# Attention over targets: one-hots turned on TensorE, maxima in two bf16 parts; a table stored from ScalarE's DMA queue

## The chip, the cores and the metric

The kernel runs on one core of a Trainium2 chip. The metric is the device time of one execution in microseconds, the median of three runs. TensorE is called PE, VectorE DVE, ScalarE ACT, GpSimd POOL and SyncE SP, as in the profile.

## The reference, cut to what matters

Four graph layers run over 12,500 nodes with 64 features and 400,000 edges, whose targets (dst) are sorted. The change touches the preparation, which all layers share, and the first layer, an attention over the edges of each target with 4 heads:

```
xl = (x @ W_l + b_l).reshape(n, 4, 16);  xr = (x @ W_r + b_r).reshape(n, 4, 16)
e = (edge_attr @ W_e).reshape(-1, 4, 16)
g = leaky_relu(xl[src] + xr[dst] + e, 0.2)
logits = einsum('ehc,hc->eh', g, att)
amax = segment_max(logits, dst)
ex = exp(logits - amax[dst]);  denom = segment_sum(ex, dst)
alpha = ex / (denom[dst] + 1e-16)
out = segment_sum(xl[src] * alpha[..., None], dst)
```

## The kernel before

The nodes lie in 98 blocks of 128. The sorted edges are cut into NG = 880 groups of 512 edges (4 tiles of 128, T = 4), each within one block, and the first layer goes over the groups in order. All five engines run their own instruction stream over the groups, software-pipelined by hand: `stage(f, lag, ...)` in a `body(g)` runs step f for group g - lag. Loops are unrolled four times (SLOTS = 4), and only semaphores tie the engines together.

**One group.** SP loads the sources, the target keys (twice: one key per partition, and as a row `key16` sent to all 128 partitions) and 16 edge features. POOL gathers 4 x 128 rows of the table `tab0` by indirect DMA. PE turns the edge features (L991), ACT copies them (L1064), PE makes their products (`feature_rows`, L1012) and adds the rows of the targets with a one-hot (`key_rows`, L1019, 12 matmuls). DVE adds the gathered rows (L893) and forms the scores (L899 to L904).

**Two one-hots.** DVE makes both in `onehots`: `ohN` (nodes x edges, bf16) in one instruction from the loaded row (L882), and `oh` (edges x nodes, f32) in four from the keys (L886). `oh` is used by `node_sums` on PE (L1035), so DVE waits for the node sums four groups back (`s_acc`) before it writes its buffer again. ACT makes a penalty from `ohN` (L1069).

**Maxima.** ACT rounds the scores to bf16 (`hi`, L1080). PE turns them to 4 rows (`turn_scores`, L997), ACT copies them (L1095) with a permuted write, PE spreads each head's row over 128 partitions (`spread`, L1007; two heads in `spread_first`, two in `spread_others`, since there are two buffers), and DVE adds the penalty and reduces (L919, four per group). The new maximum `mn` is bf16 (L926). PE takes it back to the edges (`edge_maxima`, L1027, 4 matmuls), DVE subtracts (L937, L940), ACT takes the exponent (L1090), DVE multiplies the values (L945), PE sums by node (L1035) and DVE adds to ACC (L952, L955).

**Order on PE** in `body(g)`: spread_first(g-1), node_sums(g-2), feature_rows(g+1), turn_scores(g), spread_others(g-1), key_rows(g+1), edge_maxima(g-1), turn(g+2). **Order on DVE**: scores(g), onehots(g+2), maxima(g-1), keep(g-2), exponents(g-1), local_keys(g+3), gathered(g+1), values(g-1). **Order on ACT**: high_part(g), score_rows(g), kept(g+1), weights(g-1), rescale(g-1), features(g+2), penalty(g).

POOL also scatters, between the gathers, the sorted edge records (`scatter_fill`, L1495) that later layers read.

**The preparation** finds each edge's place. SP's one DMA queue takes, in this order, a 25 MB copy of edge features, 47 stores that fill the record array (L377, 144 MB), and 14 small stores of a table of tiles (L382, two for each of 7 pieces). DVE makes these pieces (L538 to L542) in two buffers; for piece c it waits (`s_tst`) until the stores of piece c-2 have landed. After the seventh piece DVE and PE place the edges (L561 to L569), and the phase ends.

Of the kernel before, what the change touches and what calls it, by code (L numbers as in the profile page):

```python
# [18 lines left out]
F32 = mybir.dt.float32  # L19
# [10 lines left out]
T = 4  # L30
# [116 lines left out]
def program(nc, x, src, dst, ea16, ea64, rowvec, wtab0, w_e, wtab1, w2, wtab2, watt_e, wgru, bgru, w1, w3, out):  # L147
# [11 lines left out]
    with ExitStack() as top:  # L159
# [134 lines left out]
        with phase() as ctx:  # L294
# [65 lines left out]
            with nc.Block() as block:  # L360
                @block.sync
                def _(sp):
# [12 lines left out]
                    for r in range(0, NG * T, RUN):  # L375
                        m = min(RUN, NG * T - r)
                        sp.dma_start(places[:, r:r + m, :], rinit[:, 0:m, :]).then_inc(s_rec, 16)  # L377
                    for c in range(NTS):
# [4 lines left out]
                    sp.wait_ge(s_rec, 16 * n_rec)  # L383
                    sp.wait_ge(s_eap, 16)
                    for q in range(2):
                        at_least(sp, s_tst[q], 32 * ((NTS + 1 - q) // 2))
# [382 lines left out]
        def target_attention():  # L769


            table, heads, width, n_val, order = tab0, HEADS, D, D, 0
            R = table.shape[1]
            PT = PT1
            VC = n_val // heads + 1
            att = rows[:, ROWS["att"]]
            with phase() as ctx:
                def sbl(name, shape, dt=F32):
                    return sb_in(ctx, f"t_{name}", shape, dt)

                def seml(name):
                    return sem_in(ctx, f"t_{name}")

                w = sbl("w_ea", [T * DE, T, width])
                key = sbl("key", [P, SLOTS, T], I32)
                idx = sbl("idx", [P, SLOTS, T, 1], I32)
                ea = sbl("ea", [P, SLOTS, T, DE])
                row = sbl("row", [P, SLOTS, GE], I16)
                N_LOADS = 4
                G, oh, Gv = in_place_of_h(ctx, ("t_G", R), ("t_oh", P), ("t_Gv", R))  # L790
                lo = sbl("lo", [P, T])
                ohN = sbl("ohN", [P, SLOTS, GE], BF16)
                pen = sbl("pen", [P, 2, GE], BF16)
                eaT = sbl("eaT", [T * DE, P])
                z = sbl("z", [P, T, width])
                za = sbl("za", [P, T, width])
                lg = sbl("lg", [P, 2, T, heads])
                hi = sbl("hi", [P, T, heads], BF16)
                lgT = sbl("lgT", [heads, GE], BF16)
                sel = sbl("sel", [heads, heads, P], BF16)  # L800
                junk = sbl("junk", [P, 2, GE], BF16)
                gm = sbl("gm", [P, heads])
                mn = sbl("mn", [P, heads], BF16)
                df = sbl("df", [P, heads])
                corr = sbl("corr", [P, 2, heads])
                dd = sbl("dd", [P, T, heads])
                V = sbl("V", [P, T, heads, VC])
                M = sbl("M", [P, NB + 1, heads])
                ps_ea = ps_in(ctx, "t_ps_ea", [P, 512])
                ps_lT = ps_in(ctx, "t_ps_lT", [P, 2 * GE], BF16)  # L810
                ps_z = ps_in(ctx, "t_ps_z", [P, T, width])
                n_lb = 2
                ps_lb = ps_in(ctx, "t_ps_lb", [P, n_lb, GE])
                ps_m = ps_in(ctx, "t_ps_m", [P, 512])
                ps_a = ps_in(ctx, "t_ps_a", [P, 512])
                s_w, s_mi = seml("ea_weights"), seml("maxima_set")
                s_ld = [seml(f"edges_landed{k}") for k in range(SLOTS)]
                s_g = [seml(f"gathered{k}") for k in range(SLOTS)]
                (s_wz, s_lo, s_oh, s_ohN, s_pen, s_eaP, s_eaT, s_z, s_add, s_kept, s_act, s_mul, s_lg, s_hi, s_lT, s_lTc, s_sel, s_mn, s_df,
                 s_mb, s_corr, s_me, s_d0, s_d, s_p, s_V, s_acc, s_sc, s_done) = (seml(n) for n in (  # L820
                    "ea_weights_zero", "local_key", "onehot", "onehot_nodes", "penalty", "ea_turned", "ea_ready", "edge_rows",
                    "rows_added", "gathered_kept", "activated", "weighted", "score", "score_high", "score_turned", "score_rows", "selector", "new_max",
                    "max_step", "max_stored", "rescale", "edge_max", "score_less_max", "exponent", "weight", "values", "group_sums",
                    "acc_rescaled", "group_done"))
                s_lb = [seml(f"scores_spread{h}") for h in range(heads)]
                s_gm = [seml(f"group_max{h}") for h in range(heads)]
                filler = scatter_fill(ctx, 2, 0, (1, 3), (2, 0), (1, 0), ROUNDS)

                def tile_of(a, t):
                    return a.rearrange("n (p t) -> n t p", t=T)[:, t, :]  # L830

                with nc.Block() as block:
                    @block.sync
                    def _(sp):
                        sp.wait_ge(s_wz, 1)
                        for t in range(T):
                            sp.dma_start(w[t * DE:(t + 1) * DE, t, :], w_e).then_inc(s_w, 16)

                        def body(g, k, r):
                            at_least(sp, s_lo, g - SLOTS + 1)  # L840
                            at_least(sp, s_ohN, g - SLOTS + 1)
                            settle(sp)
                            at_least(sp, s_g[k], r * (16 * T))
                            at_least(sp, s_eaP, g - SLOTS + 1)
                            settle(sp)
                            e = sp.value_load(goff[0:1, bass.ds(g, 1)], min_val=0, max_val=E)
                            sp.dma_start(idx[:, k, :, 0], srcp[bass.ds(e, GE)].rearrange("(p t) -> p t", p=P)).then_inc(s_ld[k], 16)
                            sp.dma_start(row[:, k, :], key16[bass.ds(e, GE)].partition_broadcast(P)).then_inc(s_ld[k], 16)
                            sp.dma_start(key[:, k, :], keyp[bass.ds(e + 1, GE)].rearrange("(p t) -> p t", p=P)).then_inc(s_ld[k], 16)
                            sp.dma_start(ea[:, k], eap[bass.ds(e, GE), :].rearrange("(p t) c -> p t c", p=P)).then_inc(s_ld[k], 16)  # L850
                        steps(sp, NG, body, fill=lambda k, r: filler.load(sp, k, r), filled=filler.rounds)

                    @block.gpsimd
                    def _(pool):
                        def body(g, k, r):
                            pool.wait_ge(s_ld[k], (r + 1) * (16 * N_LOADS))
                            at_least(pool, s_add, g - SLOTS + 1)
                            at_least(pool, s_kept, g - SLOTS + 1)
# [4 lines left out]
                        steps(pool, NG, body, fill=lambda k, r: filler.scatter(pool, k, r), filled=filler.rounds)  # L863
                        filler.landed(pool)

                    @block.vector
                    def _(dve):
                        dve.memset(w[:], 0.0).then_inc(s_wz, 1)
                        dve.tensor_copy(sel[:], bcast(ident[0:heads, 0:heads], 2, P)).then_inc(s_sel, 1)
                        dve.memset(M[:], -LOW).then_inc(s_mi, 1)  # L870
                        dve.wait_ge(s_mi, 1)

                        def local_keys(g, k, r):
                            dve.wait_ge(s_ld[k], (r + 1) * (16 * N_LOADS))
# [1328 lines left out]
```

## Time and profile before

| | us |
|---|---|
| median of 3 runs (lowest to highest) | 25825.76 (25818.92 to 25836.37) |
| the profiled execution: its own time | 25656.45 |
| its span | 25654.3 |
| PE, DVE, ACT, POOL busy in it | 19085.9, 16571.8, 6762.4, 16256.9 |

The span is one execution from its first instruction to its last; busy time is an average over stages that have different limits. The preparation fills about the first 1050 us, the first layer's attention some 7.8 ms from 1312 us on.

### The profile page before, as it was taken

To read this page: it belongs to the slowest core of one execution; us is meant where nothing else is said; L and a number is where in the kernel's file an instruction comes from. 1 tells how busy PE (TensorE), PEld (TensorE's weight loads), DVE (VectorE), ACT (ScalarE), POOL (GpSimd) and SP (SyncE) were. 2 spreads that over 40 slices of the span, in tenths; PEclk is the share of its full clock that TensorE was granted. 3 is DMA by queue.
4 is the path that set the end of the run, shared out by engine and by line. 5 is a ranking of instruction groups with operands and counts; after the bars stand their busy time and mean duration, and the time that the engine had idled before them with its cause. 6 is when DMAs were issued, how large, how long until landed. Compare 5 with 4: busy or idle time off the path is not lost. (4 is left out here: it accounts for less than half of the span.)

```text
span 25654.3 us, 556495 instructions
## 1 busy us (share of the span) xinstructions
PE 19085.9 (74%) x100300; PEld 12086.3 (47%) x100301; DVE 16571.8 (65%) x59093; ACT 6762.4 (26%) x22440; POOL 16256.9 (63%) x16941
## 2 busy tenths in 40 slices
PE   3578888888888859999999987888888863333334
PEld 1244444444444435555555654666666633333332
DVE  4878888888888864444444556777777654444444
ACT  0033333333333322222222213444444311111111
POOL 0067777777777727777777643666666617777772
PEclk7755555555555555555555557999999855555555
DMA  7032332222233423333333365888888823333332
GB/s 300 5 62 57 57 57 57 57 57 57 57 57 57 57 37 75 76 75 76 75 75 76 70 51 95 132 131 131 129 132 132 117 35 59 59 59 59 59 59 22
DMA packets 3333220, 1984.04 MB, mean 77 GB/s; under 512 B 2469132, under 2 KB 2942196, under 8 KB 3325904
## 3 DMA queue, kind: packets, MB, share of 16 engines
q1 hardware_dynamic: 2735346, 1137.99, 22.6%
q0 software_dynamic: 597808, 845.34, 20.4%
q8 instruction: 21, 0.34, 0.0%
q14 instruction: 45, 0.37, 0.0%
HBM read 1667.63 MB, written 342.49 MB: 78 GB/s over the span
## 5 line engine op out<-in xcount | busy, mean ns | idle before, releaser
L861 POOL DMA_INDIRECT H<-tab,t_idx x3520 | 3405.6, 967 | 2300.0 <-DMA t_ea<-eap 1227.6
L1212 POOL DMA_INDIRECT H<-tab,a_rs x3520 | 3374.7, 959 | 1965.0 <-issue 1193.7
L1571 POOL DMA_INDIRECT H<-tab,m_idx x3520 | 3350.1, 952 | 1654.6 <-issue 1014.7
L1751 POOL DMA_INDIRECT g_G<-tab,g_rs x3232 | 3054.1, 945 | 1520.4 <-issue 944.5
L1495 POOL DMA_INDIRECT rec<-PT,posi x3125 | 3059.9, 979 | 1460.2 <-issue 1224.4
L1817 PE MATMUL g_ps_a<-g_zr,g_oh 128*128 128x64 f32 x6464 | 1586.4, 427 | 2620.3 <-ACT g_zr L1801 2011.6
L1817 PEld LDWEIGHTS g_ps_a<-g_zr,g_oh 128*128 128x128 f32 x6464 | 1438.7, 327 | 2768.6 <-issue 1903.5
L919 DVE CUSTOM_DVE_ANT_0 t_junk<-t_ps_lb,t_pen 128x512 bf16<-128x512 f32 x3520 | 2292.3, 689 | 555.9 <-PE t_ps_lb L1007 257.3
L1007 PE MATMUL t_ps_lb<-t_lgT,t_sel 4*128 4x512 bf16 x3520 | 1894.7, 603 | 498.5 <-DVE t_gm L919 468.6
L1671 PEld LDWEIGHTS m_ps_a<-m_Sx,H 128*128 128x128 f32 x7040 | 1565.6, 327 | 1416.0 <-issue 1415.3
L1035 PEld LDWEIGHTS t_ps_a<-t_V,H 128*128 128x128 f32 x7040 | 1567.5, 328 | 1367.1 <-issue 1367.1
L1035 PE MATMUL t_ps_a<-t_V,H 128*128 128x68 f32 x7040 | 1718.4, 426 | 590.8 <-DVE t_V L945 313.9
L1095 ACT COPY t_lgT<-t_ps_lT 4x512 bf16<-4x512 bf16 x880 | 1163.3, 1322 | 3499.2 <-PE t_ps_lb L1007 3498.5
L1781 DVE TENSOR_TENSOR ACC<-ACC,g_ps_a 128x64 f32 x3232 | 715.6, 221 | 1899.6 <-DVE ACC L1781 1524.0
L1671 PE MATMUL m_ps_a<-m_Sx,H 128*128 128x65 f32 x7040 | 1731.5, 424 | 0.5 <-ACT m_Sx L1694 0.5
L1645 PE MATMUL m_ps_m<-m_zT,w_sb 64*64 64x512 f32 x1760 | 1729.2, 1084 | 0.1
L1610 DVE TENSOR_TENSOR m_z<-m_ps_z,H 128x256 f32<-128x256 f32 x880 | 373.8, 425 | 2034.8 <-DMA H<-tab,m_idx 1300.5
L1603 DVE TENSOR_TENSOR_SCAN m_S<-H,m_S,m_ps_m 64x512 f32<-64x512 f32 x879 | 1116.1, 1270 | 795.9 <-PE m_ps_m L1645 795.8
L1317 PE MATMUL a_ps_z<-a_w_ea,a_eaT 64*128 64x288 f32 x3520 | 1101.9, 434 | 550.1 <-DVE a_z L1235 535.5
L1356 PE MATMUL a_ps_w<-PT,identb 128*128 128x432 bf16 x3524 | 1235.7, 358 | 0.0
L1689 ACT COPY m_zT<-m_ps_t 64x512 f32<-64x512 f32 x880 | 509.8, 579 | 2690.9 <-PE m_ps_t L1638 2687.2
L1638 PE MATMUL m_ps_t<-ident,m_zr 128*64 128x128 f32 x3520 | 925.3, 417 | 296.0 <-ACT m_zr L1699 294.7
(344 smaller groups left out, 37049.3 us busy)
## 6 DMA issues: line engine op xcount, KB each, us to landing
a_rs<-rec SPq DMA_DIRECT2D x880, 164.0 KB
rec<-H SPq DMA_DIRECT2D x46, 3116.0 KB
g_rs<-rec SPq DMA_DIRECT2D x3232, 41.0 KB
t_row<-key SPq DMA_DIRECT2D x880, 128.0 KB
m_row<-key SPq DMA_DIRECT2D x880, 128.0 KB
H<-startp SPq DMA_DIRECT2D x880, 128.0 KB
a_row<-keyc SPq DMA_DIRECT2D x880, 128.0 KB
PT<-in_ea SPq DMA_DIRECT2D x625, 160.0 KB
```

Source lines behind the costliest of these rows:

```text
L861: pool.indirect_dma_start(G[:, k, t, :], None, table, bass.IndirectOffsetOnAxis(ap=idx[:, k, t, :], axis=0)).then_inc(s_g[k], 16)
L919: dve.tensor_tensor_reduce(junk[:, h % 2], ps_lb[:, h % n_lb], pen[:, k % 2], 1.0, -LOW, ALU.add, ALU.max, gm[:, h:h + 1]).then_inc(s_gm[h ...
L1007: pe.matmul(ps_lb[:, h % n_lb], sel[:, h, :], lgT[:], start=True, stop=True).then_inc(s_lb[h], 1)
L1035: mm = pe.matmul(ps_a[:, 0:heads * VC], oh[:, k, t, :], V[:, t].rearrange("p h c -> p (h c)"), start=(t == 0), stop=(t == T - 1))
L1212: pool.indirect_dma_start(G[:, k % SLOTS, t, 0:R], None, tab2, bass.IndirectOffsetOnAxis(ap=rs[:, k, t, 1:2], axis=0)).then_inc(s_g[k % SL ...
L1356: pe.matmul(ps_w[:], identb[:], PT[:, 0, 0:3, :].rearrange("p s c -> p (s c)"), start=True, stop=True)
L1495: pool.indirect_dma_start(rec, bass.IndirectOffsetOnAxis(ap=self.posi[:, j, t:t + 1], axis=0), rbi[:, j, t, :], None).then_inc(self.s_sc[j ...
L1571: pool.indirect_dma_start(G[:, k, t, :], None, tab1, bass.IndirectOffsetOnAxis(ap=idx[:, k, t, :], axis=0)).then_inc(s_g[k], 16)
L1645: pe.matmul(ps_m[0:D, :], w[:], zT[:], start=True, stop=True).then_inc(s_msg, 1)
L1671: mm = pe.matmul(ps_a[:, 0:D + 1], ohL[:, k, t, :], Sx[:, t, :], start=(t == 0), stop=(t == T - 1))
L1751: pool.indirect_dma_start(G[:, k, t, :], None, tab3, bass.IndirectOffsetOnAxis(ap=rs[:, k, t, 1:2], axis=0)).then_inc(s_g[k], 16)
L1817: mm = pe.matmul(ps_a[:, q, t, 0:D], oh[:, q, t, :], zr[:, q, t, :], start=True, stop=True)
```

## The change

In the preparation the 14 stores of the table of tiles are issued by ACT instead of SP:

```diff
@@ sync
-                    for c in range(NTS):
-                        a, b = 512 * c, min(NT, 512 * c + 512)
-                        sp.wait_ge(s_ti, c + 1)
-                        for o in range(2):
-                            sp.dma_start(tiles[o:o + 1, a:b], ti[0:1, c % 2, o, 0:b - a]).then_inc(s_tst[c % 2], 16)
                     sp.wait_ge(s_rec, 16 * n_rec)
                     sp.wait_ge(s_eap, 16)
+                @block.scalar
+                def _(act):
+                    for c in range(NTS):
+                        a, b = 512 * c, min(NT, 512 * c + 512)
+                        act.wait_ge(s_ti, c + 1)
+                        for o in range(2):
+                            act.dma_start(tiles[o:o + 1, a:b], ti[0:1, c % 2, o, 0:b - a]).then_inc(s_tst[c % 2], 16)
```

`target_attention()` becomes `attention(layer, order, table, heads, width, we, n_val)`, called once, as `attention(0, 0, tab0, HEADS, D, w_e, D)`; its parts for other layers are not used. The row load is gone (3 loads instead of 4). DVE makes only the one-hot `ohb` (bf16, edges x nodes); PE turns it, and ACT makes the turned one-hot, the penalty and the f32 copy. Scores and maxima are carried as a high and a low bf16 part:

```diff
@@ DVE
-                            dve.tensor_scalar(ohN[:, k], row[:, k], base_node[...], pcol[:], ALU.subtract, ALU.is_equal).then_inc(s_ohN, 1)
                             dve.wait_ge(s_lo, g + 1)
-                            at_least(dve, s_acc, g - SLOTS + 1)
+                            at_least(dve, s_ohT, g - 1)
+                            at_least(dve, s_oh32, g - 1)
                             for t in range(T):
-                                ins = dve.tensor_scalar(oh[:, k, t, :], iota_b[:], lo[:, t:t + 1], None, ALU.is_equal)
+                                ins = dve.tensor_scalar(ohb[:, q, t, :], iota_b[:], lo[:, t:t + 1], None, ALU.is_equal)
+                        def split(g, k, r):     # after onehot(g+2), before maxima(g-1)
+                            dve.wait_ge(s_lp0, g + 1)
+                            dve.tensor_tensor(lgp[:, :, 1, :], lg[:, k % 2], lgp[:, :, 0, :], ALU.subtract).then_inc(s_lp, 1)
@@ DVE maxima
                             dve.tensor_tensor(mn[:], m_old, gm[:], ALU.max).then_inc(s_mn, 1)
                             dve.wait_ge(s_mn, g + 1)
+                            at_least(dve, s_me, g)
+                            dve.tensor_copy(mnp[:, 0], mn[:]).then_inc(s_mh, 1)
                             dve.tensor_tensor(df[:], m_old, mn[:], ALU.subtract).then_inc(s_df, 1)
                             dve.wait_ge(s_df, g + 1)
                             dve.tensor_tensor(m_old, mn[:], mn[:], ALU.max).then_inc(s_mb, 1)
+                            dve.wait_ge(s_mh, g + 1)
+                            dve.tensor_tensor(mnp[:, 1], mn[:], mnp[:, 0], ALU.subtract).then_inc(s_ml, 1)
@@ PE turn
+                            pe.wait_ge(s_oh, g + 1)
+                            at_least(pe, s_pen, g)
+                            for t in range(T):
+                                mm = pe.transpose(ps_oh[:, t, :], ohb[:, q, t, :], identb[:])
+                            mm.then_inc(s_ohT, 1)
@@ PE turn_scores
-                                mm = pe.transpose(ps_lT[0:heads, ...], hi[:, t, :], identb[:])
+                                mm = pe.transpose(ps_lT[0:2 * heads, ...], lgp[:, t]..., identb[:])
@@ PE edge_maxima
-                            pe.wait_ge(s_mn, g + 1)
+                            pe.wait_ge(s_mh, g + 1)
+                            pe.wait_ge(s_ml, g + 1)
                             for t in range(T):
-                                mm = pe.matmul(ps_m[...], tile_of(ohN[:, k], t), mn[:], start=True, stop=True)
+                                for i in range(2):
+                                    mm = pe.matmul(ps_m[...], ohN[:, k, t, :], mnp[:, i], start=(i == 0), stop=(i == 1))
@@ ACT
-                            act.activation(pen[:, k % 2], ohN[:, k], ACT.Copy, bias=-LOW, scale=LOW).then_inc(s_pen, 1)
+                        def copies(g, k, r):    # last in ACT's body, for group g+2
+                            act.wait_ge(s_ohT, g + 1)
+                            at_least(act, s_me, g - SLOTS + 1)
+                            act.copy(ohN[:, k], ps_oh[:, 0:T]).then_inc(s_ohN, 1)
+                            act.activation(pen[:, k], ps_oh[:, 0:T], ACT.Copy, bias=-BIG, scale=BIG).then_inc(s_pen, 1)
+                            at_least(act, s_acc, g - SLOTS + 1)
+                            act.wait_ge(s_oh, g + 1)
+                            act.copy(oh[:, k], ohb[:, q]).then_inc(s_oh32, 1)
-                            act.copy(lgT[:].rearrange("h (p t) -> h t p", t=T), ps_lT[0:heads, 0:GE].rearrange(...))
+                            act.copy(lgT[:], ps_lT[0:2 * heads, 0:T * P]).then_inc(s_lTc, 1)
```

The selector of `spread` has 8 rows instead of 4, two of them one, so that each head's high and low part are added.

## Rows read from the trace of the kernel before

**Rows 1.** First and last start of the node sums' matmuls, by source line:
```profile
L1035 PE MATMUL t_ps_a<-t_V,H x7040: 421/421/478, 1338.0 to 9143.1; 128*128 128x68 f32 x196
```
**Rows 2.** Windows: length, busy us (x instructions) by engine, PE clock, DMA share, GB/s:
```profile
4000.00:5000.00 1000.00, 819.29 (x3947) 448.94 (x3946) 803.72 (x2928) 320.99 (x903) 710.79 (x733) 0.50 0.30 57
10000.00:11000.00 1000.00, 932.34 (x4522) 577.25 (x4522) 497.31 (x1361) 214.64 (x530) 758.65 (x792) 0.50 0.38 75
16500.00:17500.00 1000.00, 861.37 (x6601) 627.32 (x6599) 771.08 (x3385) 423.26 (x1960) 683.87 (x714) 0.96 0.82 130
```
**Rows 3.** Waits of DVE, 4000 to 6000 us: total us, times, longest:
```profile
DVE H L886 <- PE t_ps_a L1035: 136.1, 225, 0.6
DVE t_junk L919 <- issue: 61.1, 113, 0.9
```
**Rows 4.** PE's timeline, one group: start, us, engine, line, operation, count, [idle before]:
```profile
5031.50 0.30 PE L1027 MATMUL t_ps_m<-t_mn,t_ohN 128*128 128x4 bf16 x4
5031.66 0.40 PE L991 MATMUL t_ps_ea<-ident,t_ea 128*64 128x128 f32 x1
5031.99 1.03 PE L1007 MATMUL t_ps_lb<-t_lgT,t_sel 4*128 4x512 bf16 x2
5033.84 1.95 PE L1035 MATMUL t_ps_a<-t_V,H 128*128 128x68 f32 x8 [0.82 <-DVE t_V L945]
5035.72 1.22 PE L1012 MATMUL t_ps_z<-t_w_ea,t_eaT 64*128 64x256 f32 x2
5036.86 0.59 PE L997 MATMUL t_ps_lT<-identb,t_hi 128*4 128x128 bf16 x4
5037.81 1.12 PE L1007 MATMUL t_ps_lb<-t_lgT,t_sel 4*128 4x512 bf16 x2 [0.36 <-DVE t_gm L919]
5039.20 0.97 PE L1019 MATMUL t_ps_z<-PT,t_ohN 128*128 x12 [0.26 <-issue]
5040.29 0.30 PE L1027 MATMUL t_ps_m<-t_mn,t_ohN 128*128 128x4 bf16 x4
```
**Rows 5.** DVE's timeline in the same group:
```profile
5035.90 0.88 DVE L886 TENSOR_SCALAR H<-iota_b,t_lo 128x128 f32<-128x128 bf16 x4 [0.60 <-PE t_ps_a L1035]
...
5038.57 0.69 DVE L919 CUSTOM_DVE_ANT_0 t_junk<-t_ps_lb,t_pen 128x512 bf16<-128x512 f32 x1 [0.29 <-PE t_ps_lb L1007]
...
5039.19 0.69 DVE L919 CUSTOM_DVE_ANT_0 t_junk<-t_ps_lb,t_pen 128x512 bf16<-128x512 f32 x1
...
5040.07 0.16 DVE L926 TENSOR_TENSOR t_mn<-t_M,t_gm 128x4 bf16<-128x4 f32 x1 [0.19 <-issue]
5040.27 0.17 DVE L929 TENSOR_TENSOR t_df<-t_M,t_mn 128x4 f32<-128x4 bf16 x1
...
5041.93 0.42 DVE L945 TENSOR_TENSOR t_V<-H,t_V 128x256 f32<-128x256 f32 x1
```
**Rows 6.** Two groups of ACT by line: shapes, count | busy us, mean ns | idle before:
```profile
L1095 ACT COPY t_lgT<-t_ps_lT 4x512 bf16<-4x512 bf16 x880 | 1163.3, 1322 | 3499.2 <-PE t_ps_lb L1007 3498.5 <-PE t_ps_lT L997 0.7
L1689 ACT COPY m_zT<-m_ps_t 64x512 f32<-64x512 f32 x880 | 509.8, 579 | 2690.9 <-PE m_ps_t L1638 2687.2 <-issue 3.7
```
**Rows 7.** Waits of PE in the second layer, 12000 to 14000 us:
```profile
PE m_ps_z L1653 <- issue: 28.1, 75, 0.4
```
**Rows 8.** The preparation, DVE's timeline around its long wait:
```profile
288.68 0.43 DVE L542 CAST ti<-fo 128x512 int32<-128x512 f32 x1
...
295.28 0.43 DVE L542 CAST ti<-fo 128x512 int32<-128x512 f32 x1
...
506.33 0.69 DVE L538 TENSOR_SCALAR ti<-ps_all 128x512 int32<-128x512 f32 x1 [210.23 <-DMA tiles<-ti]
```
**Rows 9.** The preparation: a window (columns of rows 2), the record stores and the last placing step:
```profile
300.00:500.00 200.00, 0.00 (x0) 0.00 (x0) 0.00 (x0) 0.00 (x0) 0.00 (x0) 0.50 1.00 430
L377 SPq DMA_DIRECT2D rec<-H x47: 433/6526/42002, 81.3 to 439.0; - x47
L569 DVE COPY_PREDICATED PT<-mask,ps_all x196: 1331/1888/2439, 566.2 to 1045.9; 128x2048 f32<-128x2048 int16 x98, 128x1077 f32<-128x1077 int16 x98
```

More of the change, by code:

```diff
@@ L767, in _, with attention @@
                         steps(act, NB, body, 2)
-        def target_attention():
-            table, heads, width, n_val, order = tab0, HEADS, D, D, 0
+        def attention(layer, order, table, heads, width, we, n_val):
             R = table.shape[1]
-            PT = PT1
+            PT = PT2 if layer == 2 else PT1
             VC = n_val // heads + 1
-            att = rows[:, ROWS["att"]]
+            v0 = R - n_val
+            banks = 1 if T * width <= 512 else 2
+            tpb = T // banks
+            att = rows[:, ROWS["att"]] if layer == 0 else rows[:, ROWS["w_att2"]]
@@ L815, in target_attention @@
[L815 to L830, printed above, removed]
+                ps_oh = ps_in(ctx, f"ps_oh{layer}", [P, 2 * T, P], BF16)
+                ps_ea = ps_in(ctx, f"ps_ea{layer}", [P, 512])
+                ps_lT = ps_in(ctx, f"ps_lT{layer}", [P, 2 * T * P], BF16)
@@ new lines, in attention @@
+                ps_z = ps_in(ctx, f"ps_z{layer}", [P, banks, 512])
+                n_lb = min(heads, 2)
+                ps_lb = ps_in(ctx, f"ps_lb{layer}", [P, n_lb, T, P])
+                ps_m = ps_in(ctx, f"ps_m{layer}", [P, 512])
+                ps_a = ps_in(ctx, f"ps_a{layer}", [P, 512])
+                zv = [ps_z[:, b, 0:tpb * width].rearrange("p (t c) -> p t c", t=tpb) for b in range(banks)]
+                s_w, s_mi, s_eac = seml("ea_weights"), seml("maxima_set"), seml("ea_together")
@@ L832, in target_attention @@
+                s_lb = [seml(f"scores_spread{h}_") for h in range(heads)]
+                if layer == 0:
+                    filler = scatter_fill(ctx, 2, 0, (1, 3), (2, 0), (1, 0), ROUNDS)
+                else:
+                    filler = None
+                s_gm = [seml(f"group_max{h}_") for h in range(heads)]
                 with nc.Block() as block:
@@ L968, in body @@
                                 blocks[1] = block_of(g - 1)
+                            stage(split, 0, NG, *at)
                             stage(maxima, 1, NG, *at)
@@ L1077, in high_part @@
                         def high_part(g, k, r):
+                            q = k % 2
+                            if layer:
+                                act.wait_ge(s_lg0, g + 1)
+                                at_least(act, s_d0, g - 1)
+                                act.activation(lg[:, q], ss[:], ACT.Identity, bias=rows[:, ROWS["b_att2"]]).then_inc(s_lg, 1)
                             act.wait_ge(s_lg, g + 1)
                             at_least(act, s_lT, g)
-                            act.copy(hi[:], lg[:, k % 2]).then_inc(s_hi, 1)
+                            act.copy(lgp[:, :, 0, :], lg[:, q]).then_inc(s_lp0, 1)
                         def rescale(g, k, r):
@@ L1099, in body @@
                             stage(score_rows, 0, NG, *at)
[L1100 removed]
+                            if layer == 0:
+                                stage(kept, -1, NG, *at)
                             stage(weights, 1, NG, *at)
@@ L1103, in body @@
                             stage(features, -2, NG, *at)
-                            stage(penalty, 0, NG, *at)
-                        for g in range(2):
-                            features(g, g, 0)
-                        kept(0, 0, 0)
-                        filler.first(act)
-                        pipeline(act, NG, body, 2, fill=lambda k, r: filler.keys(act, k, r), filled=filler.rounds)
+                            stage(copies, -2, NG, *at)
+                        features(0, 0, 0)
+                        copies(0, 0, 0)
+                        features(1, 1, 0)
+                        copies(1, 1, 0)
+                        if layer == 0:
+                            kept(0, 0, 0)
+                        if filler:
+                            filler.first(act)
+                            pipeline(act, NG, body, 2, fill=lambda k, r: filler.keys(act, k, r), filled=filler.rounds)
+                        else:
+                            pipeline(act, NG, body, 2)
         def source_attention():
```

219 lines of the change are left out of this document (133 added, 86 removed).

## The prediction

> **What bounds the kernel now.** I read the extent of the first layer's stage, then its windows, then DVE's and PE's waits, then one group on the two timelines, and last the preparation. All sums below are made against the profiled execution (span 25654.3 us, own time 25656.45); the median of the runs shown is 25825.76, 169 higher, and I put the difference on that.
>
> The stage runs from 1337.9 to 9143 us for 880 groups [rows 1]: 8.88 us a group, 30% of the span. In it PE is busy 82%, DVE 80%, POOL 71% and ACT 32% [rows 2]: no engine is full, so a loop of waits must set the pace. DVE waits in every group for the node sums, 136.1 us / 225 = 0.60 us [rows 3], and PE waits for DVE twice, 0.82 us for the values and 0.36 us for the first group maximum [rows 4]. So it is one ring over both: values, node sums on PE (1.95), one-hots on DVE, four maxima, values. Once in four groups DVE also loses up to 0.9 us for which it waits on nobody, 0.27 us a group on average [rows 3].
>
> In the preparation DVE stands still for 210.2 us until a tile store has landed [rows 8]. The window 300 to 500 us shows no instruction of a compute engine and DMA full at 430 GB/s [rows 9]. The small stores stand behind the record stores in SP's queue, the last of which starts at 439 us [rows 9]. This wait is on the path: the placing, which ends the phase at 1046 us, comes after it.
>
> **Part 1, the table of tiles.** The stores leave SP's queue. DVE's stall falls to what a store costs beside the records, which still keep DMA full until 506. The stores of piece c are needed two pieces on. A piece takes 6.6 us (288.68 to 295.28 [rows 8]), so a landing below that costs nothing. No row shows a small store beside a full queue. Bounds: from below 0 us left; from above the whole 210 us, if the stores still get through only when the records are done. The nearest row is the record store itself, 6.5 us median on the queue [rows 9]: if a small store waits for about one, a landing takes some 7 to 9 us and the five waits leave 5 to 10 us. I take 10 us left: **-200 us**. SP still waits for the records, but they end at 506 us, and the placing, moved from 1046 to some 846, covers them. ACT, which issues 14 stores, has nothing else in this stretch.
>
> The Trainium skill ("DMA: Bandwidth & Descriptors", "Queues, rings and completion order") says that each DMA engine takes turns between the queue rows that have work, a packet at a time, and SP and ACT own one row each; by that rule the stores pass the records, as I take it. The same page ("Issuing engines are not separate DMA queues") says that a second issuing engine saves only the time to issue; by that sentence alone part 1 would be worth nothing. No trace here has a transfer from ACT's queue, so neither is shown yet.
>
> **Part 2, the attention stage.** What goes: DVE's second one-hot (L882), the row load of 128 KB a group (DMA at 30% in this stage, cover enough [rows 2]: nothing), and the 0.60 us wait of DVE for the node sums, which moves to ACT, where the sums in question are long done. That breaks the ring, and a longer one takes its place, which I follow from one `edge_maxima` on PE to the next. It stays on PE up to the second pair of spreads, and goes over DVE from there:
>
> - edge_maxima, now 8 matmuls: 0.16 to the turn now [rows 4]; four take 0.30, so one more costs some 0.04: 0.16 + 0.16, with a second semaphore 0.35
> - four transposes of 128x128 bf16, new. The nearest row is turn_scores, also four with 128 moving columns, 0.59 from first start to last end [rows 4]. Taken by start to start: 0.48. Bounds 0.3 (loads and moves all overlap) and 0.9 (weights of 128 columns instead of 4 not hidden at all)
> - the feature turn to the first spread 0.33, the spread pair 1.03, a gap 0.05 [rows 4]
> - node sums to feature rows 1.88, feature rows to turn_scores 1.14 [rows 4]
> - turn_scores to the other spreads, wait left out: 0.95 now, of which 0.36 is a wait [rows 4]: 0.50 (the last end overlaps)
> - first of them to the third maximum 0.76 (37.81 to 38.57), third to fourth 0.62, fourth to `mn` 0.88 [rows 4, 5]
> - `mn` to the end of `ml`: DVE's small operations start 0.20 apart (40.07, 40.27 [rows 5]). Before, PE started 0.22 after `mn` began. Now `mh`, `df`, the stored maximum and `ml` lie between: 4 x 0.20 + 0.17 + 0.06 = 1.03
>
> The sum is 0.35 + 0.48 + 1.41 + 3.02 + 0.50 + 2.26 + 1.03 = 9.05 us. The same chain before, with its waits, is 8.79 (31.50 to 40.29 [rows 4]). In other words: 0.16 + 0.03 + 0.48 + 0.81 = 1.48 us are added to PE's chain, and some 1.22 come back, because PE no longer stands for the values (0.77) nor for the first maxima (0.45).
>
> The values must not be late in the new ring. They end 2.06 us after edge_maxima began (42.35 - 40.29 [rows 4, 5]), some 2.2 with the longer edge_maxima, and the spread pair ends 0.35 + 0.48 + 0.33 + 1.03 = 2.19 after it: just hidden. If the transposes are cheaper than I think, this wait returns and takes the gain.
>
> DVE has 7.14 us of work a group now [rows 2]. It loses one long operation and gains three of 0.17, so it stays near 7.2 of 9.05; its loop turn falls into this slack. PE's own loop turn, till now hidden behind waits, comes out: the nearest row is the second layer, 0.37 us a turn of four groups (28.1 / 75 [rows 7]), 0.1 a group. Another 0.05 is for waits that queue on PE behind `s_oh`, `s_pen` and `s_ohT`; behind these stand the feature turn and the spreads. New stage: 9.05 + 0.10 + 0.05 = 9.20 us a group, against 8.88: 0.32 x 880 = **+282 us**.
>
> ACT: now 2.85 us a group [rows 2]. It gains two copies out of PSUM and one in SBUF, 128x512 each, and moves the penalty; the score copy loses its permuted write. Prices: 0.58 for a plain copy of 512 f32 out of PSUM, 1.32 for the permuted bf16 one [rows 6]. I blame the permuted write for the 0.74 between them, so I take 0.6 each. The copies then end before DVE's scores do; `high_part`, which stands behind them on ACT and feeds DVE's new `split`, is not late. With 1.32 for the two copies out of PSUM it is; that is a rival.
>
> The Trainium skill ("ScalarE: Activation LUTs", "What ACT_TABLE_LOAD costs") gives an activation with immediate scale and bias 186 ns + 0.833 ns an element, for f32 and bf16 alike, 612 ns here. The plain copy agrees (579), the score copy does not (1322). By the rule alone the sum is mine; by the measured row it is rival B.
>
> Total: -200 + 282 = +82 us. 25825.76 + 82 gives 25908, which I round to **25900**.
>
> **The rivals.**
>
> A, faster: the new ring is no longer than the old one. Its place is PE between edge_maxima and the first spread. If transposes and the extra matmuls cost 0.35 together instead of 0.64, and `ml` starts 0.6 after `mn`, the group stays at 8.88 or falls to 8.8, and the 200 us of part 1 remain: 25560 to 25640. It decides below 0.23 us added per group (200 / 880). For it: 1.2 us of PE's waits are there to be used up. Against: four dependent starts of 0.20 can hardly be had for less.
>
> B, much slower: a bf16 read out of PSUM is what makes the score copy 1.32. Then turned one-hot and penalty cost 1.5 us more on ACT, `high_part` and `split` are late by some 0.6 to 0.8, turn_scores and the first maxima too, and a group takes some 9.7: 0.8 x 880 - 200 = +500, 26330. For it: nothing else on ACT reads bf16 there. Against: the permuted write is the more unusual part of that copy.
>
> C, much faster: PE's clock. It stands at 0.50 (1.2 GHz) throughout this stage, and at 0.50 with PE 93% busy in the second layer, but at 0.96 in the third, where PE is busy 86% [rows 2]. The transposes are more bf16 work. Should the stage go to 2.4 GHz, PE's 5.5 us of the ring halve, DVE becomes the bound at some 8.2: -0.7 x 880 - 200 = -800, 25000. Against: the new wait for `ml` opens a gap between key_rows and edge_maxima that was not there.
>
> D: the stores still wait for the records, all of part 1 is nothing, and the stage's +282 stand alone: 26110. The full DMA window [rows 9] speaks for it.
>
> **How the numbers follow.** My forecast (stage 9.1 to 9.4 a group, part 1 works; 25820 to 26080) 0.42, A 0.23, B 0.15, C 0.06, D 0.08, something slower still 0.06. Two runs of this kernel differ by under 0.2% (52 us), which is what counts as no change. The forecast's own range gives 0.30 slower, 0.12 same; A gives 0.20 faster, 0.03 same; C is faster, B, D and the rest slower: faster 0.26, same 0.15, slower 0.59. I move 0.06 from slower to faster for parts of the slack I may have missed: 0.32, 0.15, 0.53. The range takes A down to 25580 and B up to 26400.
>
> **What would show it.** Stall at L538 gone, placing done by about 850 us, and stores on ACT's queue: part 1 right. In the stage: no wait of DVE for `ps_a`, PE's waits for the values near zero, a wait of PE for `mnp` of some 0.8 us between key_rows and edge_maxima, group period 9.2. The copies out of PSUM at 0.6 on ACT, else B. Clock at 0.50, else C. I am wrong if the values still end last for the node sums, if the period stays under 9.1, or if the split is late.

## The result, and the profile after

The changed kernel takes 25441.5 us (median of 4 runs, 25411.0 to 25446.5), the kernel before 25822.3 beside it (25806.4 to 25836.4): a ratio of 0.985, interval 0.9833 to 0.9867, **381 us faster**. Forecast was 25900, 78 us slower, in a range from 25580: wrong in sign, and below the range.

The page of the profiled execution after (own time 25411.0 us), the span and one queue:

```profile
span 25409.4 us, 572084 instructions
...
q10 hardware_dynamic: 28, 0.03, 0.0%
```

The line q10 is new: ACT's queue, with 28 packets and 0.03 MB.

First the preparation, by line: the stores on ACT's queue (to [rows 8, 9]), the placing, and the node sums (to [rows 1]), with count, min/median/max ns, first and last start:

```profile
L387 ACTq DMA_DIRECT2D tiles<-ti x14: 200/236/481, 288.8 to 323.6; - x14
...
L572 DVE COPY_PREDICATED PT<-mask,ps_all x196: 1333/1886/2436, 358.9 to 837.9; 128x2048 f32<-128x2048 int16 x98, 128x1077 f32<-128x1077 int16 x98
...
L1114 PE MATMUL ps_a<-V,H x7040: 421/421/482, 1127.9 to 8713.5; 128*128 128x68 f32 x196
```

The stores go out as the pieces are made, the placing ends at 838 instead of 1046, and the attention stage begins at 1127.9 instead of 1338.0: 210 us sooner. The stage then lasts 7585.6 us instead of 7805.1: another 219.5 us, where I had forecast 282 more. The same two lines in the trace of before show what the old queue did:

```profile
L382 SPq DMA_DIRECT2D tiles<-ti x14: 214/253/8346, 445.7 to 530.9; - x14
...
432.08 13.56 SPq L377 DMA_DIRECT2D rec<-H  x2
445.69 70.12 SPq L382 DMA_DIRECT2D tiles<-ti  x8
```

The first store's data was ready at 289 [rows 8]; SP could issue it only at 445.7, after it had got rid of its last record store, and the stores that DVE waits for had landed at 506. So some 157 us passed before the issue, and 60 more while the records still filled DMA. DVE stood still from 296.1 on (506.33 - 210.23), so 150 of its 210 us lie before the issue.

Now the stage itself: one window (columns of [rows 2]), and PE's and DVE's waits from 4000 to 6000 us (total us, times, longest):

```profile
4000.00:5000.00 1000.00, 855.89 (x4976) 493.01 (x4976) 808.25 (x3246) 367.37 (x1159) 730.74 (x754) 0.50 0.22 44
```

```profile
PE ps_m L1106 <- DVE mnp L984: 274.2, 232, 1.3
PE ps_z L1096 <- issue: 13.6, 58, 0.2
...
DVE junk L975 <- PE ps_lb L1082: 204.4, 231, 1.2
```

No wait of DVE for the node sums, none of PE for the values; PE waits for `mnp` in every group, 1.18 us on average. The clock is still 0.50. The same on the timeline, one group from `edge_maxima` to `edge_maxima` (to [rows 4, 5]):

```profile
5001.57 0.16 DVE L981 TENSOR_TENSOR mn<-M,gm 128x4 f32<-128x4 f32 x1 [0.20 <-issue]
5001.77 0.17 DVE L984 CAST mnp<-mn 128x4 bf16<-128x4 f32 x1
5001.85 0.15 DVE L986 TENSOR_TENSOR df<-M,mn 128x4 f32<-128x4 f32 x1
5002.04 0.16 DVE L988 TENSOR_TENSOR M<-mn 128x4 f32 x1
5002.12 0.15 DVE L990 TENSOR_TENSOR mnp<-mn,mnp 128x4 bf16<-128x4 f32 x1
5002.23 0.23 DVE L1014 TENSOR_TENSOR ACC<-ACC,corr 128x68 f32 x1
...
5002.37 0.35 PE L1106 MATMUL ps_m<-mnp,ohN 128*128 128x4 bf16 x8 [1.31 <-DVE mnp L984]
...
5002.60 0.58 PE L1057 MATMUL ps_oh<-identb,ohb 128*128 128x128 bf16 x4
...
5002.98 0.42 PE L1065 MATMUL ps_ea<-ident,ea 128*64 128x128 f32 x1
...
5003.34 1.03 PE L1082 MATMUL ps_lb<-lgT,sel 8*128 8x512 bf16 x2
...
5003.64 0.41 DVE L1007 TENSOR_TENSOR V<-H,V 128x256 f32<-128x256 f32 x1
5003.68 0.58 ACT L1149 COPY ohN<-ps_oh 128x512 bf16<-128x512 bf16 x1
...
5004.16 0.59 ACT L1151 ACTIVATE pen<-ps_oh 128x512 bf16<-128x512 bf16 x1
...
5004.30 1.98 PE L1114 MATMUL ps_a<-V,H 128*128 128x68 f32 x8
...
5006.20 1.22 PE L1088 MATMUL ps_z<-w_ea,eaT 64*128 64x256 f32 x2
...
5007.35 0.59 PE L1072 MATMUL ps_lT<-identb,lgp 128*8 128x128 bf16 x4
...
5007.87 1.03 PE L1082 MATMUL ps_lb<-lgT,sel 8*128 8x512 bf16 x2
...
5008.65 0.69 DVE L975 CUSTOM_DVE_ANT_0 junk<-ps_lb,pen 128x512 bf16<-128x512 f32 x1 [1.16 <-PE ps_lb L1082]
...
5009.27 0.69 DVE L975 CUSTOM_DVE_ANT_0 junk<-ps_lb,pen 128x512 bf16<-128x512 f32 x1
...
5010.17 0.17 DVE L981 TENSOR_TENSOR mn<-M,gm 128x4 f32<-128x4 f32 x1 [0.20 <-issue]
...
5010.98 0.35 PE L1106 MATMUL ps_m<-mnp,ohN 128*128 128x4 bf16 x8 [1.32 <-DVE mnp L984]
```

It is the ring that I had drawn, in the order that I had drawn, with the period 8.61 instead of 9.20 us (8.59 to 8.70 over the four groups of a loop turn; the stage gives 8.62). From `mn` (5001.57) the two halves of DVE's little chain can be read: the high part of `mnp` after 0.20, but `df`, which needs only `mn`, already 0.08 behind it, and the low part 0.08 behind the stored maximum.

The two spans differ by only 245 us. The parts above make 430; 170 are lost again in the third layer, which the change does not touch: its node sums run 4968.1 us in the profiled execution before and 5138.0 after. Some 15 more are lost elsewhere.

```profile
L1349 PE MATMUL a_ps_a<-H x7040: 217/275/422, 15701.4 to 20669.5; 128*128 128x65 f32 x196
```

```profile
L1446 PE MATMUL a_ps_a<-H x7040: 217/275/422, 15285.0 to 20423.0; 128*128 128x65 f32 x196
```

### The profile page after: what moved, and what is told of

It is laid out like the page before. It is cut to its first block and busy times, and to the rows that moved or that the text cites. A ratio compares the mean times of both kernels' runs of the same rounds, so it can differ in the third digit from the quotient of the medians.

```text
span 25409.4 us, 572084 instructions
## 1 busy us (share of the span) xinstructions
PE 19250.5 (76%) x107313; PEld 12397.8 (49%) x107341; DVE 16439.5 (65%) x60853; ACT 7048.7 (28%) x24200; POOL 16250.5 (64%) x16941
## 5 line engine op out<-in xcount | busy, mean ns | idle before, releaser
L897 POOL DMA_INDIRECT H<-tab,idx x3520 | 3403.9, 967 | 2091.5 <-issue 1062.4
L975 DVE CUSTOM_DVE_ANT_0 junk<-ps_lb,pen 128x512 bf16<-128x512 f32 x3520 | 2292.5, 689 | 824.4 <-PE ps_lb L1082 779.0
L1114 PEld LDWEIGHTS ps_a<-V,H 128*128 128x128 f32 x7040 | 1567.2, 328 | 766.2 <-issue 766.2
L1082 PE MATMUL ps_lb<-lgT,sel 8*128 8x512 bf16 x3520 | 1828.9, 614 | 0.2 <-DVE gm L975 0.2
L1114 PE MATMUL ps_a<-V,H 128*128 128x68 f32 x7040 | 1731.0, 427 | 11.6 <-DVE V L1007 6.5
L1185 ACT COPY lgT<-ps_lT 8x512 bf16<-8x512 bf16 x880 | 506.1, 575 | 2962.5 <-PE ps_lb L1082 2961.3
```

Source lines behind the costliest of these rows:

```text
L897: pool.indirect_dma_start(G[:, k, t, :], None, table, bass.IndirectOffsetOnAxis(ap=idx[:, k, t, :], axis=0)).then_inc(s_g[k], 16)
L975: dve.tensor_tensor_reduce(junk[:, h % 2].rearrange("p t e -> p (t e)"), ps_lb[:, h % n_lb].rearrange("p t e -> p (t e)"), pen[:, k].rearr ...
L1082: pe.matmul(ps_lb[:, h % n_lb].rearrange("p t e -> p (t e)"), sel[:, h, :], lgT[:], start=True, stop=True).then_inc(s_lb[h], 1)
L1114: mm = pe.matmul(ps_a[:, 0:heads * VC], oh[:, k, t, :], V[:, t].rearrange("p h c -> p (h c)"), start=(t == 0), stop=(t == T - 1))
```

## The experiments

The runs were made in three groups, each with runs of the kernel before beside them: 1 to 4 (on the chip that the record numbers 15), 5 to 8, and 9 to 12 some 25 minutes later (both on the number 6). "Stage" is the extent of the node sums, first start to last start.

**1. The stores alone.** The kernel before, with the 14 stores issued by ACT as in the diff above.

> The kernel before, with only the 14 stores of the table of tiles issued from ScalarE's DMA queue. Theory (queue): the stores pass the record stores, DVE's stall of 210.2 us at the third piece is gone, the node sums of the first layer start at 1128 instead of 1338, the stage itself still takes 7805 us: -210 us. Rival (the same DMA engines are full, so the stores wait as before): no change. If the two parts don't add up, this and the next run show by how much.

25775.7 us against 25979.8: ratio 0.9925 (0.9908 to 0.9941), -204. The stage, by line:

```profile
L1038 PE MATMUL t_ps_a<-t_V,H x7040: 421/421/478, 1132.2 to 8935.4; 128*128 128x68 f32 x196
```

It begins 206 us sooner than [rows 1] and lasts as long (7803.2).

**2. The attention alone.** The changed kernel, with the stores back on SP.

> The changed kernel, with the 14 stores back on SyncE's queue: the attention part alone. Theory (ring): the stage takes 7586 us instead of 7805, 8.62 instead of 8.88 us a group, the stall of 210 us stays: -220 us. Rival (my recorded sum): the ring with its new terms is 9.2 us a group, +280 us.

25750.0 us: ratio 0.9918 (0.9902 to 0.9935), -230. Stage 7579.3 us, from 1337.8 on. DVE's waits in the preparation hold the old stall:

```profile
DVE ti L538 <- DMA tiles<-ti: 211.7, 1, 211.7
```

The two halves add: -204 and -230 make -434, and the profiled execution after gave -430 up to the end of this stage. The whole change measured -381, some 50 less; the third layer's time, which differs between executions, may hold that, but no run shows it. Both halves are gains, so the step that failed is the stage's sum.

**3. The old ring opened without the new one.** In the kernel before, only the f32 one-hot, which waited for the node sums, is made one body later, so that these are long done. Nothing goes to PE or ACT, no value is split (lines shortened):

```diff
-                        def onehots(g, k, r):   # both, for g+2
+                        def onehots(g, k, r):   # only ohN, for g+2
+                            dve.wait_ge(s_ld[k], (r + 1) * (16 * N_LOADS))
                             dve.tensor_scalar(ohN[:, k], row[:, k], ...).then_inc(s_ohN, 1)
+
+                        def onehots32(g, k, r): # s_lo, s_acc, four tensor_scalar
...
+                            stage(onehots32, -1, NG, *at)
...
-                            stage(local_keys, -3, NG, *at)
+                            stage(local_keys, -2, NG, *at)
```

> The kernel before, with the f32 one-hots made one body later on DVE (group g+1 instead of g+2 in body g, the local keys with them), so that the buffer that they overwrite was read a whole body ago; no work is added or removed, nothing is turned on PE, no parts are split. Theory (ring): the pace of before was the ring values -> node sums -> one-hots; with it broken DVE's wait for ps_a of 0.60 us is gone and the period falls from 8.88 to some 8.3 us (then POOL's 6.5 transfers a group of 1.27 us each, or DVE with some 8.0, is the bound): -500 us. Rival (the gain came from DVE having less to do and from the cheaper score copy): no change, 8.88 us a group.

25494.0 us: ratio 0.9818 (0.9802 to 0.9834), -486, twice what the change's whole attention part gives. Stage 7311.9 us, 8.32 a group. POOL's waits from 4000 to 6000 us, and the window:

```profile
POOL H L861 <- issue: 286.6, 940, 0.3
...
POOL rec L1500 <- issue: 182.9, 600, 0.3
```

```profile
4000.00:5000.00 1000.00, 852.32 (x4207) 472.86 (x4207) 843.63 (x3129) 346.55 (x965) 761.85 (x782) 0.50 0.33 61
```

DVE no longer waits for the node sums, so the old ring was what [rows 3, 4] said. What bounds now is, by its own time, an engine I had left out: POOL works 761.85 us of the window and stands 0.30 us between every two of its 782 indirect transfers, 235 us more. That is 997 of 1000. It hardly waits for anybody (7 us in 2000); at 6.5 transfers a group, 0.97 + 0.30 us each, it needs 8.3 us. No run takes transfers away, so this bound is read from the trace and not tested.

**4. The score copy.** In the kernel before, ACT writes `lgT` in order and reads PSUM permuted, instead of the reverse:

```diff
-                            act.copy(lgT[:].rearrange("h (p t) -> h t p", t=T), ps_lT[...].rearrange("h (t p) -> h t p", t=T))
+                            act.copy(lgT[:].rearrange("h (p t) -> h p t", t=T), ps_lT[...].rearrange("h (t p) -> h p t", t=T))
```

> The kernel before, with the copy of the turned scores on ScalarE walking its elements in the order of its output (written in a row, read from PSUM in strides) instead of the order of its input. Theory (the strided write is what cost 1.32 us against 0.58 of a plain copy): the copy takes about 0.6 us; off the ring it gains nothing, 8.88 us a group, no change within 0.2%. Rival (the copy is on the path from the spreads of one group to those of the next): 0.3 to 0.7 us a group less, -260 us or more. If the read's stride costs as much as the write's, the copy stays at 1.3 us and nothing can change.

25972.6 us: ratio 0.9999 (0.9989 to 1.0009), no change. The copy, by line:

```profile
L1095 ACT COPY t_lgT<-t_ps_lT 4x512 bf16<-4x512 bf16 x880 | 506.3, 575 | 3501.3 <-PE t_ps_lb L1007 3500.7 <-PE t_ps_lT L997 0.7
```

575 ns instead of 1322 [rows 6]: the permuted write made all of the difference. Still bf16 and still out of PSUM, so rival B's reason is refuted, and the copy is off the ring.

**5 to 8.** The same kernels as 9 to 12, in the second group of runs, 25 minutes earlier. In it all kernels ran 38 to 42% longer, the one before too (35563.6 us). In run 5 DVE stood still for 4.9 us on average about once a group (149 times, 735 us in all, from 4000 to 6000 us), in turns at two lines. No trace was kept of the kernel before beside these runs. Two of the stops, at one of the lines, two groups apart (timeline):

```profile
4002.40 0.17 DVE L996 TENSOR_TENSOR dd<-lg,ps_m 128x16 f32<-128x16 f32 x1 [4.92 <-remote]
...
4029.07 0.17 DVE L996 TENSOR_TENSOR dd<-lg,ps_m 128x16 f32<-128x16 f32 x1 [4.75 <-remote]
```

> The changed kernel, with DVE making the low part of the new maximum straight after the high part, ahead of the step and the stored maximum; nothing else moved. In the changed kernel edge_maxima starts 0.81 us after mn. Theory (the pace is now PE's ring, with this stretch of DVE in it): edge_maxima starts some 0.62 us after mn, the period falls from 8.62 to 8.43 us, the stage from 7586 to about 7420 us. Rival (PE or DVE is bound by its own work, or the values end last): the stage stays at 7586 within 20 us.

> The changed kernel, with PE turning the four one-hot tiles twice in a row (the same result written twice). In the changed kernel the four took 0.38 us from first start to the next instruction's. Theory (PE's ring without slack): the period rises by the whole of four more, 0.38 to 0.43 us, the stage to some 7930 to 7960 us. Rival (PE has slack ahead of the values, since edge_maxima starts late): less than half of that, below 7760 us. Should the added bf16 work raise PE's granted clock, it will stand above 0.50 in the stage and the period will fall.

> The changed kernel without the low part of the maxima: DVE does not make it, PE takes only the high part back to the edges (4 matmuls instead of 8) and does not wait for it. Theory (ring): edge_maxima starts 0.42 us after mn instead of 0.81, the ring is 8.62 - 0.39 - 0.05 = 8.18 us, but POOL's transfers allow no less than some 8.3 us a group (6.5 of 1.27 us): the stage takes 7300 to 7340 us, as in the kernel with the one-hot made later. Rival (the low part costs only its own 0.08 us on DVE): 7500 us or more.

> The kernel before with the two things that the runs point to and nothing else of the change: the f32 one-hots a body later on DVE, and the 14 stores of the table of tiles on ScalarE's queue. Theory: the gains add up, -486 and -204 us, that is -690 us or 2.65%, with the stage at 7312 us and the start of its node sums at 1132 us. Rival (the shift in time brings them into each other's way, or later stages give it back as they wait on POOL's records): less than -600 us.

Ratios: 0.999 (0.998 to 1.0001), 1.0215 (1.0195 to 1.0235), 0.9813 (0.9793 to 0.9832), 0.9715 (0.9699 to 0.9731). They have the order of the runs below, but with the stops none of the expected extents could be read, so the four were run again. The expectations below speak of "the chip of e5 to e8" and of stops "once per turn of its loop". The record has one chip number for both groups, so it isn't shown that the chip was another one, and a loop turn is four groups, so the stops come oftener.

**9. The low part sooner.** In the changed kernel the low part of the maximum is made right behind the high one:

```diff
                             dve.tensor_copy(mnp[:, 0], mn[:]).then_inc(s_mh, 1)
+                            dve.wait_ge(s_mh, g + 1)
+                            dve.tensor_tensor(mnp[:, 1], mn[:], mnp[:, 0], ALU.subtract).then_inc(s_ml, 1)
                             dve.tensor_tensor(df[:], m_old, mn[:], ALU.subtract).then_inc(s_df, 1)
```

> The kernel of e5 again: on the chip of e5 to e8 every engine stood still for some 5 us once per turn of its loop, in the kernel before too, which hid what the edit does; between those stops the period was 8.49 or 8.72 us, against 8.60 and 8.66 in the changed kernel. Theory (PE's ring, with DVE's stretch from mn to the low part in it): without the stops the stage takes about 7420 us, 8.43 us a group. Rival (another wait takes its place): 7540 to 7590 us.

25279.3 us against 25666.0: ratio 0.9855 (0.9835 to 0.9874), the changed kernel's own ratio. Stage 7599.4 us: my theory's gain is not there, and the rival's 7540 to 7590 is all but met. The timeline:

```profile
4015.51 0.16 DVE L981 TENSOR_TENSOR mn<-M,gm 128x4 f32<-128x4 f32 x1 [0.20 <-issue]
...
4015.71 0.17 DVE L984 CAST mnp<-mn 128x4 bf16<-128x4 f32 x1
4015.92 0.16 DVE L986 TENSOR_TENSOR mnp<-mn,mnp 128x4 bf16<-128x4 f32 x1
4016.00 0.15 DVE L988 TENSOR_TENSOR df<-M,mn 128x4 f32<-128x4 f32 x1
...
4016.18 0.36 PE L1106 MATMUL ps_m<-mnp,ohN 128*128 128x4 bf16 x8 [1.18 <-DVE mnp L984]
...
4017.71 0.41 DVE L1007 TENSOR_TENSOR V<-H,V 128x256 f32<-128x256 f32 x1
...
4018.36 1.55 PE L1114 MATMUL ps_a<-V,H 128*128 128x68 f32 x6 [0.18 <-DVE V L1007]
```

`edge_maxima` does begin sooner, 0.67 after `mn` instead of 0.81 (4016.18 - 4015.51). But three of the four operations behind `mn` now wait for the one just before, where it was two, so all that DVE does behind them comes later, the values too, and the node sums wait for the values. The four groups of a loop turn differ a little, so they are compared place by place: the values begin 2.21, 2.20, 2.39 and 2.24 us after `mn` against 2.06, 2.13, 2.31 and 2.17 in the changed kernel, and the node sums 2.73, 2.85, 2.90 and 2.75 against 2.73, 2.79, 2.82 and 2.74 (from 4006.95 and from 4000.30 us on). What `edge_maxima` gains is lost before the node sums.

**10. Turned twice.** In the changed kernel the four transposes are done twice:

```diff
-                            for t in range(T):
+                            for t in [*range(T), *range(T)]:
```

> The kernel of e6 again, for the same reason; between the stops its period was 9.00 to 9.04 us. Theory (PE's ring without slack): the stage takes 7930 to 7960 us, 0.39 us a group above the changed kernel's 8.62. Rival (slack ahead of the values): below 7760 us.

25597.6 us: ratio 0.9975 (0.9964 to 0.9985). Stage 7926.4 us, 0.39 a group above the changed kernel, for four transposes that took 0.38 to 0.43. On PE's timeline they stand in the ring at full price:

```profile
4025.96 0.35 PE L1106 MATMUL ps_m<-mnp,ohN 128*128 128x4 bf16 x8 [1.31 <-DVE mnp L984]
4026.18 1.01 PE L1057 MATMUL ps_oh<-identb,ohb 128*128 128x128 bf16 x8
4026.99 0.42 PE L1065 MATMUL ps_ea<-ident,ea 128*64 128x128 f32 x1
...
4034.96 0.35 PE L1106 MATMUL ps_m<-mnp,ohN 128*128 128x4 bf16 x8 [1.31 <-DVE mnp L984]
```

The period is 9.00, and PE's wait for `mnp` is unchanged although PE is behind by 0.4: DVE went along, as it must in a ring of both.

**11. No low part.** In the changed kernel `edge_maxima` uses the high part of the maximum alone; the low part is not made:

```diff
-                            dve.wait_ge(s_mh, g + 1)
-                            dve.tensor_tensor(mnp[:, 1], mn[:], mnp[:, 0], ALU.subtract).then_inc(s_ml, 1)
...
-                            pe.wait_ge(s_ml, g + 1)
```

> The kernel of e7 again, for the same reason; between the stops its period was 8.28 or 8.52 us. Theory (ring, then POOL's transfers as the floor): the stage takes 7300 to 7340 us, 8.3 us a group. Rival: 7450 us or more, as the mean of 8.28 and 8.52 says (8.40 x 880 = 7390 lies between).

25066.2 us: ratio 0.9771 (0.9752 to 0.9791). Stage 7405.0 us, 8.41 a group: between theory and rival, at 0.21 of the 0.3 expected. One group shows where the rest stayed:

```profile
4010.16 0.16 DVE L981 TENSOR_TENSOR mn<-M,gm 128x4 f32<-128x4 f32 x1 [0.20 <-issue]
...
4010.60 0.27 PE L1102 MATMUL ps_m<-mnp,ohN 128*128 128x4 bf16 x4 [0.96 <-DVE mnp L984]
...
4012.17 0.41 DVE L1005 TENSOR_TENSOR V<-H,V 128x256 f32<-128x256 f32 x1
...
4012.82 1.97 PE L1110 MATMUL ps_a<-V,H 128*128 128x68 f32 x8 [0.24 <-DVE V L1005]
```

`edge_maxima` begins 0.42 to 0.45 after `mn`, as expected, and PE's wait for `mnp` falls from 1.18 to 0.81 us:

```profile
PE ps_m L1102 <- DVE mnp L984: 191.8, 238, 1.0
```

But now the values come last: the node sums begin 2.44 to 2.68 after `mn` against 2.73 to 2.82, only 0.19 sooner on average.

**12. Both simple parts.** The kernel before with experiments 1 and 3: ACT's stores and the later f32 one-hot, nothing of the attention part of the change.

> The kernel of e8 again, for the same reason. Theory: the gains of e3 and e1 add up: -690 us or 2.65% (ratio 0.9735), the stage at 7312 us from 1132 us on. Rival: less than -600 us.

24959.9 us (24938.8 to 24979.7): ratio 0.973 (0.9714 to 0.9746), **-706**. The sum of 1 and 3 is -690: they add. The stage lasts 7312.3 us (1137.3 to 8449.6). It beats the kernel before and, by ratio, the changed one (0.985).

## Why the prediction was wrong

**Part 1 was right.** -200 forecast, -204 and -210 measured; the placing was done at 838 ("about 850"). The ten microseconds I left for the five waits were not there: DVE's only waits among the pieces are for PE. The Trainium skill ("DMA: Bandwidth & Descriptors", "Queues, rings and completion order") has each DMA engine take turns between the queue rows that have work, and experiment 1 agrees. The Trainium skill (the same page, "Issuing engines are not separate DMA queues") says that only the time to issue is saved, which is usually small; here it was the larger piece, 150 of the 210 us of the stall, and the measurement decides. Rival D, "the stores still wait for the records", is refuted: no piece waited for a store, although the seven pieces, made from 287 to 323 us, fell into a time when DMA was full (window, changed kernel):

```profile
200.00:400.00 200.00, 101.91 (x355) 48.96 (x357) 148.72 (x170) 0.00 (x0) 0.00 (x0) 0.74 1.00 429
```

**Part 2 had the mechanism and missed the sum.** The old ring was real (experiment 3), the new one is the one I named, with PE's work in it at full price (experiment 10). The step that failed is the sum of the new ring's terms, which made it 9.20 us a group where 8.62 were measured, and so forecast a loss of 282 us where 219.5 were gained. Its terms, forecast against the timeline above:

| term of the sum | forecast | measured |
|---|---|---|
| edge_maxima to the transposes | 0.35 | 0.23 |
| four transposes | 0.48 | 0.38 |
| feature turn to the first spread | 0.33 | 0.36 |
| spread pair, gap | 1.08 | 0.96 |
| node sums, feature rows | 3.02 | 3.05 |
| turn_scores to the other spreads | 0.50 | 0.52 |
| to the third, fourth maximum, `mn` | 2.26 | 2.30 |
| `mn` to edge_maxima | 1.03 | 0.81 |
| PE's loop turn | 0.10 | 0 |
| waits behind the new semaphores | 0.05 | 0 |
| sum | 9.20 | 8.61 |

What was copied from rows is right to 0.04, the spread pair with its gap apart. What was new is too dear in every line: 0.59 us a group (0.12 + 0.10 + 0.22 + 0.10 + 0.05), 519 us over 880 groups, against an error of 502 in the stage.

- *"DVE's small operations start 0.20 apart."* This term failed most, by 0.22. [Rows 5] show 40.07 and 40.27, an operation that waits for the one before. Of the four behind `mn` only two do, the high part and the stored maximum (0.20 and 0.19 after it); `df` and the low part wait for results that are older, and start 0.08 behind. The diff shows which is which: `df` needs `mn`, the low part needs `mn` and the high part, never the operation just before. The forecast's "four dependent starts of 0.20 can hardly be had for less" against rival A was this same error. The Trainium skill ("VectorE: DVE Perf Modes", "The DRAIN you can't avoid") says that a semaphore after each of eight copies costs nothing extra, and also that a next operation that is not held starts earlier; for these small ones the trace has 0.20 with a wait for the operation before and 0.08 without.
- *edge_maxima 0.35.* I doubled the start distance of four matmuls (0.16) and added 0.03 for a second semaphore. Eight need 0.23, only 0.07 more than four.
- *Transposes 0.48*, from `turn_scores` as the nearest row. They take 0.38 from start to start, about 0.10 each. The weights of 128 columns that I feared (bound 0.9) are hidden.
- *The spread pair 1.03* is a duration; from start to start it is 0.96, since the next matmul starts before the modelled end. Beside it I had put a gap of 0.05 that isn't there.
- *PE's loop turn.* It is there, 13.6 us in 58 turns, but at `key_rows`. At that place the ring runs over DVE's maxima and PE has 1.3 us to spare, so it costs next to nothing. I had priced it without asking where in the ring it falls.
- *The extra 0.05.* Beside the loop turn PE waits for nothing but `mnp`.

**The slack of the values was judged rightly**: "just hidden", though both of its terms were too large: the values end 1.7 to 1.9 us after `edge_maxima` began (forecast 2.2), and the node sums could begin 1.9 to 2.0 after it (2.19). The node sums don't wait in the changed kernel, and do as soon as `edge_maxima` comes 0.1 us sooner (experiments 9 and 11). So moving the low part gives nothing, and leaving it out gives half of what it takes from the ring, 0.21 of 0.39.

**Rival A was the right one**, with its mechanism (the ring no longer than before) and its price too small: 8.62 a group instead of 8.8 to 8.88. The transposes and the extra matmuls cost 0.45 together, more than the 0.35 that it asked for; the low part begins 0.55 after `mn`, as it asked. **B** is refuted: the copies out of PSUM take 577 and 595 ns. The Trainium skill ("ScalarE: Activation LUTs", "What ACT_TABLE_LOAD costs") gives 612 for them, which agrees within 6%, for the score copy as well once its write is contiguous (575). **C** did not occur: the clock stayed at 0.50, 1.2 GHz, with PE 86% busy in the window.

**Chances.** Every new term stood on a nearest row that was dearer than the thing itself, so the errors had one sign and added. The low end of the range stood on rival A at 8.8 a group, 0.18 above what was measured. One row was misread without entering the sum: DVE waits on nobody in every second group (113 of 225 [rows 3]), not once in four.

**The 169 us** between the profiled execution and the median of before were put on the difference unchanged. In profiled executions the third layer's stage, the same code, took 5268 to 5299 us in runs 1 to 4 and 4974 to 5002 in runs 9 to 12, and the kernel before took 25980 beside the first and 25666 beside the second. That the gap is this stage fits, but timed runs leave no trace, so it is argued and not shown; nor was it tried why the stage varies.

## What to carry to other kernels

When two engines wait for each other across a reused buffer, first write that buffer one body later: here that gave more than rebuilding the producers did. Price a new ring by starts, term by term, dependent and independent operations apart, and a loop turn only if it falls on the engine that holds the ring at that place. Then look for the next bound before trusting the gain: an engine at 76% busy can be full if there is a gap before every instruction of it. Small stores that someone waits for don't belong behind bulk stores in one queue, where they can't even be issued.

## What the runs showed of the hardware

- ACT's write of 512 bf16 with a stride of four elements took 1322 ns, in order 575; a permuted read of PSUM cost nothing (575).
- In the chain behind `mn`, DVE's operations on 128x4 start 0.08 us after the one before if they don't wait for it, 0.18 to 0.21 if they do.
- POOL's indirect transfers stand 0.30 us apart even if nothing is waited for, so 782 of them with 762 us of work fill 1000 us.
- SP could issue its first small store (about 1 KB a packet: 0.03 MB in 28) only 157 us after the data was ready, behind its own record stores.
- In runs 5 to 8 all kernels ran 38 to 42% longer; in run 5 DVE stood still for some 5 us about once a group, in stops most of which the trace puts on no engine's work. The Trainium skill ("Runtime: NRT & Kernel Launch", "Instruction fetch mechanics") says that a taken branch to code outside the fetched pages forces a fetch; the stops come oftener than the loop turns, no run here shows what was fetched, and the same kernels did not stop in runs 9 to 12, so the cause stays open.
